# Expert rows in units of 128, two experts split ahead, narrow blocks interleaved, O's low half ahead of the maxima

## Chip, cores and metric

The kernel runs on one core of one Trainium2 chip. The metric is the device time of one execution in microseconds. The engines are PE (matmul; PEld its weight loads), DVE, ACT, POOL and SP; each works through its own queue in order, and semaphores join them. DMAs are issued from the queues of SP, ACT and POOL.

## What is computed

For x of 4 batches x 1024 tokens x 256, the reference adds to x an attention output times a gate that a mixture of experts makes. Both start from the same normalized input.

```python
x = L0_attn_x
xn = _layernorm(x)
s = attention(xn)              # 8 heads of 128, one shared K and V, causal, position added to q and k
logits = xn @ router_w + router_b          # 8 experts, the two largest are kept
gating = softmax(kept logits)
h = relu(einsum('td,edh->eth', xn, w1) + b1)      # H = 1024
y = einsum('eth,ehd->etd', h, w2) + b2
g = silu(einsum('etd,te->td', y, gating))
return x + s * g
```

Only the two chosen experts of a token count, so the kernel gathers rows by expert: 4096 tokens x 2 = 8192 rows.

## The kernel before

Every float32 operand of a large product is split in two float16 halves, high and low (PASSES: high x high, high x low, low x high), so each product of 128 x 128 weights is three matmuls.

`prologue` (lines 300 to 750) loads x in pairs of tiles (p = 0 to 15, two tiles of 128 tokens each). Per pair, DVE normalizes, ACT makes the high half, POOL (even p) or DVE (odd p, BY_DVE) the low half, PE turns both and makes the router's logits, and ACT or DVE (six p, OUT_DVE) copies the turned tile out of PSUM. In the second half of this loop ACT and POOL also scale and split the weights of expert 0 (`weights`, 8 pieces of 128 x 512). Then comes the routing, all on DVE and PE in one chain: `choose` twice (the two largest logits), `counts` on PE (33 matmuls that leave in psR for each token the number of rows of each expert ahead of it, and the totals), `blocks` (blocks of each expert and where they start), `ranks` and `slots` (a row number for each token and choice), `one_hots` with `place` on PE (the inverse: which token stands in each row), `owners` (blk_e, the expert of each block), and who, the list of tokens by row. A block has BLK = 256 rows of one expert, and 39 blocks (NBLK) are enough for any counts. POOL then gathers 128 rows at a time (`gather`, an indirect DMA), SP turns the first four (`straight`) and stores the others (`keep`) in a table in memory, from where ACT later loads them turned (`load`). A part ends when all engines have passed its end, POOL's drain (a wait for its own work) among them.

`experts` (lines 756 to 912) takes the blocks in order. For block n and each of 8 groups g of 128 hidden units, PE runs `up(n, g)` and `down(n - 1, g)`, six matmuls each, ACT adds the bias and makes relu, DVE splits the result, and DVE and ACT bring out the rows of block n - 2. The weights of the block's expert are addressed through a register that is loaded from blk_e, and PE waits for w_done (8 pieces for each expert) at a block's start. POOL alternates one gather and the split of one piece (`split`: scale, high, low); SP alternates `keep` and `stage` (the piece's load). AHEAD = 8 gathers lie in the prologue.

`attention` (lines 915 to 1424) has 32 heads of five steps k. In each step PE makes the scores of a group of query tiles and, from the previous head, one of four `values` (the product with V, in two PSUM banks by turns), and sometimes a projection (a job) or an output tile. DVE does reciprocals(k-1), maxima(k), the low half of a job, `o_low` (the low half of a values result, which frees its bank), and `low(k-2)` of the probabilities. ACT does a job's high half, exponentials, and `o_high`, the high half of a values result, ahead of `o_low`.

## Time and profile before

| | us |
|---|---|
| median of 3 runs | 1158.84 (1158.31 to 1159.88) |
| profiled execution | 1160.2 |
| its span | 1158.4 |
| PE busy in it | 1041.3 (90%) |
| DVE busy | 889.6 (77%) |
| ACT busy | 553.7 (48%) |
| POOL busy | 521.3 (45%) |

The busy shares are means over three parts with different limits, so they are read by stretch. All readings are from one execution; the difference between its time and its span, 1.8 us, lies around the program. A time of the trace counts from the span's start. The form "[0.61 <-DVE b_outs L1276]" behind a row is the idle time of its engine just before it, and what ended it.

### The profile page before, as it was taken

Reading aid. Unit: us, or ns where it says so; the run is one execution under the profiler, and the core shown is the slowest. Engines: PE = TensorE matmul, PEld = TensorE weight load, DVE = VectorE, ACT = ScalarE, POOL = GpSimd, SP = SyncE. Lnnn points to the kernel's source line nnn. Section 1 sums busy time; section 2 is a strip of 40 time slices with the busy share of each in tenths; the row PEclk is TensorE's granted clock in tenths of the full one; section 3 lists DMA queues with packets and bytes.
Section 4 is the critical chain, followed back from the end, with each engine's and each line's share of the span. In section 5 each row is a group of like instructions: output and inputs, shape, how many; then the busy total and the mean of one; then the engine's idle time right before and its main releaser. Section 6 shows DMA issues by size and latency. Waiting matters only on the chain.

```text
span 1158.4 us, 28653 instructions
## 1 busy us (share of the span) xinstructions
PE 1041.3 (90%) x10419; PEld 839.2 (72%) x10419; DVE 889.6 (77%) x1570; ACT 553.7 (48%) x1251; POOL 521.3 (45%) x546
## 2 busy tenths in 40 slices
PE   2554999999999999998888989999999999999997
PEld 1443888888888888875666667767777677767776
DVE  7772676777666644448989999998989898999981
ACT  3701233323333333326666766665656665756640
POOL 1506999999986500002333334332434333434441
PEclk9966999999999999999999999999999999999999
DMA  7336578766666732226998999988899879999994
GB/s 267 115 140 169 160 178 177 180 170 174 178 177 152 142 66 56 47 74 93 165 150 143 147 159 169 164 146 150 143 179 174 147 141 152 150 166 158 156 172 107
DMA packets 412137, 172.41 MB, mean 149 GB/s; under 512 B 352730, under 2 KB 402212, under 8 KB 411364
## 3 DMA queue, kind: packets, MB, share of 16 engines
q1 hardware_dynamic: 350064, 127.97, 56.5%
q10 hardware_dynamic: 55124, 23.99, 9.2%
q0 software_dynamic: 6816, 18.62, 8.5%
q8 instruction: 90, 1.47, 0.6%
q14 instruction: 43, 0.35, 0.1%
HBM read 52.29 MB, written 32.51 MB: 73 GB/s over the span
## 4 chain that ended last, share of the span: by engine, by line
DVE 27%; PE 21%; ACT 2%; DMA 2%; issue 2%; SPq 0%; ACTq 0%; DVEq 0%
DVE b_nmax L1229 9%; DVE b_ph L1268 8%; PE b_psO L1052 7%; PE b_psS L1033 5%; PE b_psJ L1066 5%; DVE b_outs L1276 3%; DVE b_psJ L1238 2%; DMA b_pT<-b_ph 2%; DVE b_Q L1252 2%; PE b_psS L1077 2%; PE b_psS L990 2%; ACT b_ph L1164 1%; DVE b_f L1282 1%; ACT b_pr L1132 1%; PE b_psJ L990 1%
## 5 line engine op out<-in xcount | busy, mean ns | idle before, releaser
L1357 POOL TENSOR_SCALAR b_ph<-b_pr,b_rrec 128x896 f16<-128x896 f32 (+4 forms) x160 | 136.3, 859 | 469.4 <-DVE b_rrec L1258 446.0
L861 ACT ACTIVATE h<-psU,bias 128x256 f32<-128x256 f32 x312 | 129.1, 471 | 317.6 <-PE psU L809 193.7
L809 PE MATMUL psU<-bxT,w_p 128*128 128x256 f16 x1872 | 255.7, 274 | 17.8 <-issue 17.8
L1132 ACT ACTIVATE b_pr<-b_psS,b_nmax 128x1024 f32<-128x1024 f32 (+7 forms) x256 | 187.0, 735 | 142.6 <-DVE b_nmax L1229 139.2
L822 PE MATMUL psY<-w_p,hp 128*128 x1872 | 254.1, 273 | 0.0
L1052 PE MATMUL b_psO<-b_pT,b_vp 128*128 128x128 f16 x3456 | 216.1, 220 | 37.0 <-DVE b_outs L1276 26.4
L1052 PEld LDWEIGHTS b_psO<-b_pT,b_vp 128*128 128x128 f16 x3456 | 198.3, 98 | 52.5 <-DVE b_outs L1276 37.8
L879 DVE CAST hp<-h 128x512 f16<-128x512 f32 x156 | 98.0, 628 | 158.0 <-ACT h L861 147.7
L1033 PE MATMUL b_psS<-b_kp,b_Q 128*128 128x512 f16 (+3 forms) x1152 | 218.7, 326 | 0.1
L809 PEld LDWEIGHTS psU<-bxT,w_p 128*128 x1872 | 183.9, 98 | 40.2 <-issue 18.3
L1268 DVE SCALAR_TENSOR_TENSOR b_ph<-b_pr,b_rrec,b_ph 128x1024 f16<-128x1024 f32 (+7 forms) x256 | 208.0, 843 | 0.0
L1229 DVE TENSOR_REDUCE b_nmax<-b_psS 128x1 f32<-128x1024 f32 (+7 forms) x256 | 182.1, 742 | 25.3 <-PE b_psS L1036 25.3
L822 PEld LDWEIGHTS psY<-w_p,hp 128*128 128x128 f16 x1872 | 183.2, 98 | 21.2
L1033 PEld LDWEIGHTS b_psS<-b_kp,b_Q 128*128 128x128 f16 x1152 | 103.1, 98 | 77.8 <-issue 1.0
L881 DVE TENSOR_TENSOR hp<-h,hp 128x512 f16<-128x512 f32 x156 | 140.2, 899 | 5.4
L153 POOL DMA_INDIRECT rowx<-xn_split,who x78 | 86.6, 1111 | 56.7 <-DVE who L697 30.5
...
L1164 ACT ACTIVATE b_ph<-b_pr,b_rrec 128x1024 f16<-128x1024 f32 (+2 forms) x96 | 78.7, 853 | 2.0 <-DVE b_rrec L1258 2.0
L225 POOL TENSOR_TENSOR w_p<-wstage,w_p 128x512 f16<-128x512 f32 x56 | 74.4, 1329 | 4.8
L1154 ACT ACTIVATE b_Q<-b_psJ,bias 128x512 f16<-128x512 f32 x59 | 40.5, 687 | 63.2 <-DVE b_psJ L1238 62.4
L1276 DVE SCALAR_TENSOR_TENSOR b_outs<-b_psO,bias,b_outs 128x256 f16<-128x256 f32 x128 | 60.5, 473 | 12.6 <-ACT b_outs L1141 12.5
L1141 ACT ACTIVATE b_outs<-b_psO,bias 128x256 f16<-128x256 f32 x128 | 60.3, 471 | 19.7 <-PE b_psO L1052 19.6
(169 smaller groups left out, 1032.7 us busy)
## 6 DMA issues: line engine op xcount, KB each, us to landing
...
b_pT<-b_ph SPq DMA_TRANSPOSE x256
...
```

Source lines behind the costliest of these rows:

```text
L809: mm = eng.matmul(psU[w % U][:, g % 2, :].rearrange("p (t r) -> p t r", t=2), weight(n, a * W1 + c * H + g * P, P), bxT[n % 3][:, :, 2 * b ...
L822: mm = eng.matmul(psY[n % 2][:, t, :], hp[n % 2][:, a, g, t * P:(t + 1) * P], weight(n, 2 * W1 + (2 * g + b) * D, D), start=(g == 0 and k ...
L861: a = eng.activation(h32[w % 4][:, g, :], psU[w % U][:, g, :], ACT.Relu, bias=bias[:, ds(e * HT + 2 * q + g, 1)], scale=1.0 / WS)
L879: eng.tensor_copy(hp[n % 2][:, 0, sl, :], h32[w % 4][:, :, :]).then_inc(hh_, 1)
L881: eng.tensor_tensor(hp[n % 2][:, 1, sl, :], h32[w % 4][:, :, :], hp[n % 2][:, 0, sl, :], ALU.subtract).then_inc(hl_, 1)
L1033: mm = eng.matmul(dst, Q[n % 3][:, a, u * P:(u + 1) * P], kb[:, c, lo:lo + w], start=(kk == 0), stop=(kk == 2 and not last))
L1052: mm = eng.matmul(psO[w % 2][:, (u % 2) * P:(u % 2 + 1) * P], vb[:, a, j, :], pT[u][:, c * (u + 1) + j, :], start=(j == 0 and kk == 0), st ...
L1132: a = eng.activation(pr[k % 3][:, o:o + w], psS[BUF[i]][:, :, :].rearrange("p a n -> p (a n)")[:, o:o + w], ACT.Exp, bias=nmax[:, at:at + ...
L1229: a = eng.tensor_reduce(nmax[:, at:at + 1], psS[BUF[i]][:, :, :].rearrange("p a n -> p (a n)")[:, o:o + w], AX.X, ALU.max, negate=True)
L1268: a = eng.scalar_tensor_tensor(ph[k % 4][:, 2 * o + w:2 * o + 2 * w], pr[k % 3][:, o:o + w], rrec[:, at:at + 1], ph[k % 4][:, 2 * o:2 * o ...
L1276: eng.scalar_tensor_tensor(o[:, 1], psO[(4 * n + s) % 2][:, 0:2 * P], bias[:, B_V:B_V + 1], o[:, 0], ALU.add, ALU.subtract).then_inc(al_, 1)
L1357: a = eng.tensor_scalar(ph[k % 4][:, 2 * o:2 * o + w], pr[k % 3][:, o:o + w], rrec[:, at:at + 1], 1.0, ALU.mult, ALU.mult)
```

## The change

- Rows come in units of 128. An expert's rows are cut in pairs of units (blocks of 256), and a rest of 1 to 128 rows is one single unit. All pairs come first in expert order (TWIN = 31 slots), then all singles. There are 71 units and NBLK = 40 blocks, 31 of 256 rows and 9 of 128. `blocks`, `ranks` and `owners` do the arithmetic for this. Where there are more than 31 pairs, the rest are two single units each.
- `counts`: two matmuls give the totals by tile, DVE copies them, and three matmuls with a table (tri16) give the same numbers as the 33.
- Low halves of x are all DVE's, and ACT copies all turned tiles but two. The weights of experts 0 and 1 are split in the prologue and just behind it: ACT makes the high halves behind the loop, DVE the low halves (`first_low`), eight behind who and eight at the start of `experts`. POOL's splits begin with expert 2 (FIRST = 16).
- `slots` handles both choices at once, and the eight one-hots follow in a row; `gates` goes ahead of `blocks`.
- Four gathers and two turned loads stay in the prologue; the others open the expert part. The load of block 2 follows block 0's relu.
- `narrow(n, g)`: in narrow blocks two up matmuls (128 columns) alternate with one down matmul of the block before. The expert registers of these are loaded ahead, two in a block.
- In `attention`, `o_low` stands ahead of `maxima`.

```diff
-    NBLK = 2 * N // BLK + E - 1
-    UNITS = NBLK * BLK // P
-    C_TH, C_BL = C_E + E, C_E + E + MOST
-    C_LN, C_TK = C_BL + UNITS, C_BL + UNITS + P
-    CW = C_TK + NT
+    TWIN = N // P - 1
+    UNITS = 2 * N // P + E - 1
+    NBLK = UNITS - TWIN
...
+    def units_of(n):
+
+        return (2 * n, 2 * n + 1) if n < TWIN else (n + TWIN,)
+
+    def loaded(n):
+
+        return sum(16 * len(units_of(k)) for k in range(2, n + 1) if k % 3 == n % 3)
...
+    def first_low(eng, q):
+
+        hi, lo, _ = halves(q)
+        eng.wait_ge(wh0_, q + 1)
+        eng.scalar_tensor_tensor(lo, raw_of(q), WS, hi, ALU.mult, ALU.subtract).then_inc(wd_, 1)
...
-    BY_DVE = tuple(p for p in range(TWOS) if p % 2)
-    OUT_DVE = tuple(p for p in range(TWOS) if p % 8 in (1, 4, 6))
+    OUT_DVE = (TWOS - 3, TWOS - 1)
...
-                eng.matmul(psR[:, 0:NT * E], up16[:, :], M16[:, :], start=True, stop=False)
-                eng.matmul(psR[:, NT * E:], one16[:, :], M16[:, 0:E], start=False, stop=False)
-                for m in range(NT):
-                    to = NT + (m > 0)
-                    mm = eng.matmul(psR[:, (m + 1) * E:to * E].rearrange("p (n e) -> p n e", e=E), one16[:, :],
-                                    M16[:, m * E:(m + 1) * E].unsqueeze(1).to_broadcast([P, to - m - 1, E]),
-                                    start=False, stop=(m == NT - 1))
-                mm.then_inc(s_cnt, 1)
+                for h in range(PARTS):
+                    mm = eng.matmul(psJ[:, h * P:(h + 1) * P], M16[:, h * P:(h + 1) * P], one16[:, :], start=True, stop=True)
+                mm.then_inc(s_tot, 1)
+                eng.wait_ge(s_tab, 4)
+                eng.wait_ge(s_t16, 1)
+                for h in range(PARTS):
+                    eng.matmul(psR, tot16[:, h * P:(h + 1) * P], tri16[:, h, :], start=(h == 0), stop=False)
+                eng.matmul(psR[:, 0:NT * E], up16[:, :], M16[:, :], start=False, stop=True).then_inc(s_cnt, 1)
...
-                hi, _, rows = halves(q)
-                full = w_raw[:, q, :]
-                if rows:
-                    full = full.rearrange("p (g d) -> p g d", d=rows)
-                eng.activation(hi, full, ACT.Copy, scale=WS).then_inc(s_wh, 1)
-                eng.activation(full, full, ACT.Copy, scale=WS).then_inc(s_ws, 1)
-
-            eng.dma_start(c_sb[:, :], cst).then_inc(s_c, 16)
+                eng.activation(halves(q)[0], v["raw_of"](q), ACT.Copy, scale=WS).then_inc(wh0_, 1)
...
-                    if p >= 8:
-                        weights(p - 8)
...
+            for q in range(PIECES):
+                weights(q)
             eng.wait_ge(s_diff, 1)
             eng.activation(ex[:, 0, :], ex[:, 2, :], ACT.Exp).then_inc(s_e, 1)
+            for q in range(PIECES, 2 * PIECES):
+                weights(q)
             eng.dma_start(pe_sb[:, :], pe).then_inc(s_pe, 16)
...
-                if p - 1 in BY_DVE:
+                if 0 <= p - 1 < TWOS:
...
+                for j in range(2):
+                    link(eng.tensor_tensor(cm[:, j], c_sb[:, C_TH + j * MOST:C_TH + (j + 1) * MOST].unsqueeze(1).to_broadcast([P, E, MOST]),
+                                           cnt.unsqueeze(2).to_broadcast([P, E, MOST]), ALU.is_lt))
+                link(eng.tensor_reduce(nbl[:, :, :], cm, AX.X, ALU.add))
+                link(eng.tensor_tensor(nbl[:, 0, :], nbl[:, 0, :], nbl[:, 1, :], ALU.subtract))
...
+                step(eng.scalar_tensor_tensor(slot[:, :, :], row(se[0][:, 1, :]), float(BLK), rank, ALU.mult, ALU.add))
+                link(eng.tensor_tensor(cand[:, :, :], rank, row(lim[:, :]), ALU.is_ge))
+                link(eng.tensor_tensor(cand[:, :, :], cand[:, :, :], row(move[:, :]), ALU.mult))
+                link(eng.scalar_tensor_tensor(slot[:, :, :], cand[:, :, :], float(P), slot[:, :, :], ALU.mult, ALU.add))
...
+            eng.wait_ge(s_tot, 1)
+            eng.tensor_copy(tot16[:, :], psJ[:, 0:PARTS * P]).then_inc(s_t16, 1)
+            gates()
             blocks()
             ranks()
-            slots(0)
-            eng.wait_ge(s_tab, 3)
-            for s in range(CHUNKS // 2):
-                one_hots(s)
-            slots(1)
-            for s in range(CHUNKS // 2, CHUNKS):
+            slots()
+            eng.wait_ge(s_tab, 4)
+            for s in range(CHUNKS):
                 one_hots(s)
             owners()
-            gates()
             eng.wait_ge(s_sp, 1)
             eng.tensor_scalar(who[:, :], psJ[:, 0:UNITS], float(T * 2), None, ALU.add).then_inc(v["who_"], 1)
+            for q in range(PIECES):
+                v["first_low"](eng, q)
...
-            for n in range(v["AHEAD"]):
+            for n in range(4):
...
+            for n in range(2):
                 v["straight"](eng, n)
-            for n in range(4, v["AHEAD"]):
-                v["keep"](eng, n)
...
+            for n in range(2, 4):
+                v["straight"](eng, n)
+            for n in range(4, AHEAD):
+                v["keep"](eng, n)
             eng.dma_start(b2b[:, :], b2.rearrange("e d -> (e d)").partition_broadcast(P)).then_inc(b_l, 16)
-            p = PIECES + 2
-            for n in range(AHEAD, UNITS):
+            for n in range(AHEAD, AHEAD + 4):
+                v["keep"](eng, n)
+            p = FIRST + 2
+            for n in range(AHEAD + 4, UNITS):
...
+            def narrow(n, g):
+
+                w = PAIR * n + g // 2
+                if g % 2 == 0:
+                    eng.wait_ge(rl_, w - U + 1)
+                    eng.wait_ge(hl_, w - PAIR + 1)
+                for k in range(3 * DC):
+                    a, b = PASSES[k // DC]
+                    c = k % DC
+                    mm = eng.matmul(psU[w % U][:, g % 2, 0:P], weight(n, a * W1 + c * H + g * P, P), bxT[n % 3][:, 0, 2 * b + c, :],
+                                    start=(k == 0), stop=(k == 3 * DC - 1))
+                    if k == 3 * DC - 1 and g % 2:
+                        mm.then_inc(up_, 1)
+                    if k % 2:
+                        a, b = PASSES[k // 2]
+                        mm = eng.matmul(psY[(n - 1) % 2][:, 0, :], hp[(n - 1) % 2][:, a, g, 0:P],
+                                        weight(n - 1, 2 * W1 + (2 * g + b) * D, D),
+                                        start=(g == 0 and k == 1), stop=(g == HT - 1 and k == 3 * DC - 1))
+                if g == HT - 1:
...
+                    if TWIN < n < NBLK:
+                        narrow(n, g)
+                    elif n < NBLK:
                         up(n, g)
-                    if n:
+                    if n and n <= TWIN:
                         down(n - 1, g)
-                    if g == PAIR and n + 1 < NBLK:
-                        es.append(expert(eng, n + 1))
+                    elif n == NBLK and g % 2:
+                        down(n - 1, g // 2)
+                    known = min(NBLK, n + 2 + max(0, n + 11 - TWIN))
+                    if g in (2, PAIR) and len(es) < known - (g == 2):
+                        es.append(expert(eng, len(es)))
...
+                if n == 0:
+                    v["load"](eng, 2)
...
+            for q in range(PIECES, FIRST):
+                v["first_low"](eng, q)
...
-            p = PIECES
-            for n in range(AHEAD, UNITS):
+            for n in range(4, AHEAD + 4):
                 v["gather"](eng, n)
-                if p == 2 * PIECES:
-                    eng.wait_ge(v["xk_"], 48)
+            p = FIRST
+            eng.wait_ge(wd_, FIRST)
+            eng.wait_ge(v["xk_"], 48)
+            for n in range(AHEAD + 4, UNITS):
+                v["gather"](eng, n)
...
+                if k <= LAST and (k - 1) // 5 >= 1 and (k - 1) % 5:
+                    o_low((k - 1) // 5 - 1, (k - 1) % 5 - 1)
                 if k < LAST:
                     maxima(k)
                 if k - 1 in jobs.at:
                     job_low(jobs.at[k - 1])
-                if k <= LAST and (k - 1) // 5 >= 1 and (k - 1) % 5:
-                    o_low((k - 1) // 5 - 1, (k - 1) % 5 - 1)
...
```

PE's queue in the expert part, before, a piece within a block (psU is the up product, psY the down product; ISA is a register operation for the weights' address):

```order
L809 ISA
L809 MATMUL psU<-bxT_66,w_p 128x256 x3
L809 ISA
L809 MATMUL psU<-bxT_66,w_p 128x256
L809 ISA
L809 MATMUL psU<-bxT_66,w_p 128x256
L822 ISA
L822 MATMUL psY<-w_p,hp_1104 128x256
L822 ISA
L822 MATMUL psY<-w_p,hp_1104 128x256 x2
L822 ISA
L822 MATMUL psY<-w_p,hp_1104 128x256
```

After, in a narrow block:

```order
L886 ISA
L886 MATMUL psU<-bxT_67,w_p 128x128
L886 ISA
L886 MATMUL psU<-bxT_67,w_p 128x128
L892 ISA
L892 MATMUL psY<-w_p,hp_1078 128x256
L886 MATMUL psU<-bxT_67,w_p 128x128 x2
L892 ISA
L892 MATMUL psY<-w_p,hp_1078 128x256
L886 ISA
L886 MATMUL psU<-bxT_67,w_p 128x128
L886 ISA
```

The down matmul of the block before now stands behind every second up matmul, and the up matmuls have half the columns.

POOL's queue around the end of the prologue, before (rowx are the gathered rows, wstage and w_p the piece of weights before and behind the split; the two branches are the end of one part and the start of the next):

```order
L153 DMA rowx_64<-xn_split,who 128x512
L153 DMA rowx_61<-xn_split,who 128x512
L153 DMA rowx_62<-xn_split,who 128x512
L153 DMA rowx_63<-xn_split,who 128x512
L153 DMA rowx_64<-xn_split,who 128x512
L303 UNCONDITIONAL_BRANCH
L902 UNCONDITIONAL_BRANCH
L153 DMA rowx_61<-xn_split,who 128x512
L221 ISA
L221 TENSOR_SCALAR wstage_59<-wstage_59 128x512
L223 CAST w_p<-wstage_59 128x512
L225 TENSOR_TENSOR w_p<-wstage_59,w_p 128x512
```

After:

```order
L171 DMA rowx_62<-xn_split,who 128x512
L171 DMA rowx_63<-xn_split,who 128x512
L171 DMA rowx_64<-xn_split,who 128x512
L339 UNCONDITIONAL_BRANCH
L985 UNCONDITIONAL_BRANCH
L171 DMA rowx_61<-xn_split,who 128x512
L171 DMA rowx_62<-xn_split,who 128x512
L171 DMA rowx_63<-xn_split,who 128x512
L171 DMA rowx_64<-xn_split,who 128x512
L171 DMA rowx_61<-xn_split,who 128x512
L171 DMA rowx_62<-xn_split,who 128x512
L171 DMA rowx_63<-xn_split,who 128x512
```

Four gathers moved behind the end, and eight gathers stand ahead of the first split.

DVE's queue in a head of the attention part, before, the third and fourth of its five steps (b_nmax are the maxima, b_outs the low half of O, b_ph the low half of the probabilities, b_Q that of a projection):

```order
L1258 RECIPROCAL b_rrec<-b_rsum 128x2
L1229 TENSOR_REDUCE b_nmax<-b_psS 128x1 x2
L1252 SCALAR_TENSOR_TENSOR b_Q_22317<-b_psJ,bias,b_Q_22317 128x512
L1276 SCALAR_TENSOR_TENSOR b_outs_22333<-b_psO,bias,b_outs_22333 128x256
L1268 SCALAR_TENSOR_TENSOR b_ph_22319<-b_pr_22344,b_rrec,b_ph_22319 128x896
L1268 SCALAR_TENSOR_TENSOR b_ph_22319<-b_pr_22344,b_rrec,b_ph_22319 128x128
L1258 RECIPROCAL b_rrec<-b_rsum 128x2
L1229 TENSOR_REDUCE b_nmax<-b_psS 128x1
L1276 SCALAR_TENSOR_TENSOR b_outs_22333<-b_psO,bias,b_outs_22333 128x256
L1268 SCALAR_TENSOR_TENSOR b_ph_22320<-b_pr_22342,b_rrec,b_ph_22320 128x768
```

After:

```order
L1343 RECIPROCAL b_rrec<-b_rsum 128x2
L1361 SCALAR_TENSOR_TENSOR b_outs_22547<-b_psO,bias,b_outs_22547 128x256
L1314 TENSOR_REDUCE b_nmax<-b_psS 128x1 x2
L1337 SCALAR_TENSOR_TENSOR b_Q_22531<-b_psJ,bias,b_Q_22531 128x512
L1353 SCALAR_TENSOR_TENSOR b_ph_22533<-b_pr_22558,b_rrec,b_ph_22533 128x896
L1353 SCALAR_TENSOR_TENSOR b_ph_22533<-b_pr_22558,b_rrec,b_ph_22533 128x128
L1343 RECIPROCAL b_rrec<-b_rsum 128x2
L1361 SCALAR_TENSOR_TENSOR b_outs_22547<-b_psO,bias,b_outs_22547 128x256
L1314 TENSOR_REDUCE b_nmax<-b_psS 128x1
L1353 SCALAR_TENSOR_TENSOR b_ph_22534<-b_pr_22556,b_rrec,b_ph_22534 128x768
```

The low half of O moved from behind the maxima and the projection to the place behind the reciprocals.

## Rows read from the trace of the kernel before

**Rows 1.** Busy time by stretch, three parts: us, PE, PEld, DVE, ACT, POOL, clock, DMA.

```profile
0.00:103.27 103.27, 36.33 (x420) 31.54 (x420) 65.45 (x174) 33.59 (x59) 27.70 (x31) 0.83 0.51 169
...
103.27:513.90 410.63, 410.55 (x3744) 367.02 (x3744) 257.16 (x350) 129.11 (x312) 255.69 (x265) 1.00 0.57 139
...
513.90:1158.40 644.50, 594.44 (x6256) 440.68 (x6256) 566.97 (x1046) 390.97 (x880) 237.94 (x251) 0.99 0.90 152
```

**Rows 2.** PE in time (start, us, engine, line): matmuls by width, register operations.

```profile
54.03 0.83 PE L412 MATMUL a_psX<-a_rw_p,a_xT 128*128 128x8 f16 x24
...
737.93 1.35 PE L1052 MATMUL b_psO<-b_pT,b_vp 128*128 128x128 f16 x21 [0.61 <-DVE b_outs L1276]
...
739.11 2.78 PE L1066 MATMUL b_psJ<-b_wo,b_outs 128*128 128x256 f16 x24
...
741.73 1.46 PE L1033 MATMUL b_psS<-b_kp,b_Q 128*128 128x512 f16 x6
...
L809 PEldq FUSED_REGOPS  x1248: 46/46/51, 103.2 to 505.8; - x179
```

**Rows 3.** POOL, the line that ends the split of one piece of weights.

```profile
L225 POOL TENSOR_TENSOR w_p<-wstage,w_p x56: 1152/1394/1482, 105.1 to 339.9; 128x512 f16<-128x512 f32 x56
```

**Rows 4.** Timeline of DVE and ACT, second half of the normalization loop.

```profile
38.59 0.68 DVE L566 TENSOR_TENSOR a_xp<-a_x_all,a_xp 128x512 f16<-128x512 f32 x1
...
39.19 1.37 DVE L560 TENSOR_SCALAR a_x_all<-a_x_all,a_mv,a_rs 128x256 f32<-128x256 f32 x4
...
45.09 3.52 DVE L560 TENSOR_SCALAR a_x_all<-a_x_all,a_mv,a_rs 128x256 f32<-128x256 f32 x4
...
47.16 0.63 ACT L460 ACTIVATE a_xp<-a_x_all 128x512 f16<-128x512 f32 x1 [0.63 <-DVE a_x_all L560]
...
48.59 0.62 ACT L472 ACTIVATE w_p<-a_w_raw 128x512 f16<-128x512 f32 x1
...
55.87 0.42 DVE L590 SCALAR_TENSOR_TENSOR a_L<-a_psX,a_rbb 128x256 f32<-128x256 f32 x1 [2.12 <-PE a_psX L412]
```

**Rows 5.** Timeline of the routing, from the counts to who.

```profile
62.16 3.65 PE L426 MATMUL a_psX<-a_M,a_one 128*128 128x248 f16 x32
...
65.85 0.17 DVE L615 COPY a_nbl<-a_psX 128x8 f32<-128x8 f32 x1 [3.97 <-PE a_psX L426]
...
68.26 0.42 DVE L632 TENSOR_TENSOR a_cand<-a_oh,a_slot 128x256 f32<-128x256 f32 x1
...
85.77 0.23 DVE L697 TENSOR_SCALAR who<-a_psJ 128x78 uint32<-128x78 f32 x1
```

**Rows 6.** Timeline from the gathers to the first expert matmul; POOL's drain.

```profile
90.82 0.94 POOL L153 DMA_INDIRECT rowx<-xn_split,who  x1 [0.30 <-issue]
...
95.08 0.94 POOL L153 DMA_INDIRECT rowx<-xn_split,who  x1 [0.78 <-DMA bxT<-rowx]
...
97.58 0.95 POOL L153 DMA_INDIRECT rowx<-xn_split,who  x1 [0.30 <-issue]
...
103.27 7.63 PE L809 MATMUL psU<-bxT,w_p 128*128 128x256 f16 x54 [17.82 <-issue]
...
L303 POOLq DRAIN  x1: 4706/4706/4706, 96.9 to 96.9; - x1
```

**Rows 7.** Three heads by stretch; two rows of one head; DVE's waits from 600 to 1100.

```profile
559.93:577.09 17.16, 15.41 (x165) 10.87 (x164) 16.60 (x32) 11.88 (x27) 7.24 (x7) 1.00 1.00 159
...
724.97:743.28 18.31, 17.70 (x189) 13.22 (x188) 17.11 (x32) 11.89 (x27) 7.47 (x9) 1.00 1.05 158
...
743.28:763.49 20.21, 19.01 (x195) 13.83 (x194) 18.50 (x35) 12.46 (x28) 7.37 (x9) 1.00 0.86 150
...
731.49 0.47 ACT L1141 ACTIVATE b_outs<-b_psO,bias 128x256 f16<-128x256 f32 x1
...
731.64 0.17 DVE L1258 RECIPROCAL b_rrec<-b_rsum 128x2 f32<-128x2 f32 x1 [0.56 <-ACT b_pr L1132]
...
DVE b_nmax L1229 <- PE b_psS L1036: 23.0, 36, 1.1
```

214 lines of the change are left out of this document (122 added, 92 removed).

## The prediction

> **What bounds the kernel now.** I read the stretches first [rows 1]. The program has three parts in a row: a prologue of 103.3 us, an expert part of 410.6 us, an attention part of 644.5 us. In the expert part PE is busy 410.55 of 410.63 us: it is bound by PE alone, and every column of matmul taken out there is time taken out, until another engine comes late. In the prologue no engine is full (DVE 65 of 103 us), so its length is a chain of waits. In the attention part PE (92%) and DVE (88%) share the bound, and the waits between them count. The profiled execution took 1160.2 us with a span of 1158.4; the median of the runs is 1158.84. I take the differences from the trace and subtract them from the median.
>
> **Expert part.** Before, the 8192 (token, expert) pairs lie in 39 blocks of 256 rows. Each costs 48 up and 48 down matmuls of 256 columns. The spacing of such matmuls is (741.73 - 739.11)/24 = 0.1092 us [rows 2], so a block is 96 x 0.1092 = 10.48 us, and 39 are 408.8 us; the 1.8 us left of 410.6 is the slow clock of the first block. After, there are 31 blocks of 256 and 9 of 128 rows. A narrow block has 48 up matmuls of 128 columns and 24 down matmuls of 256 (128 rows instead of 256). For 128 columns with new weights each time the trace has 21 matmuls in 739.11 - 737.93 = 1.18 us, or 0.0562 us each [rows 2]. Narrow block: 48 x 0.0562 + 24 x 0.1092 = 5.32 us. Sum after: 31 x 10.48 + 9 x 5.32 = 372.8, plus 1.8: 374.6. **Gain 36.0 us**; I take 35, for seams.
>
> Can PE's queue feed narrow matmuls? Their addresses depend on the expert's number, and between them stand register operations of 46 ns [rows 2], four for six up matmuls, two more for three down ones: 6 x 0.046 = 0.28 us for each of the eight groups of a narrow block. The nine matmuls with their weight loads take the queue at most 9 x 0.035 us (24 pairs of 8 columns in 0.83 us [rows 2]) = 0.31. Together 0.59, against 0.66 us of streaming: just hidden, and the change alternates two narrow and one wide matmul, so that the load is even. The trace shows no such mix at 128 columns. Its bounds: all of the 0.28 us hidden, 5.3 us a block; none of it hidden, 5.32 + 8 x 0.28 = 7.6 us, or 20 us more for nine blocks. I take the first, since in blocks of 256 columns eight operations a group leave the spacing at 0.109.
> The Trainium skill, page "TensorE: Matmul & The Clock Gate", section "Back-to-back issue gap", speaks against this: it gives about 81 ns for each matmul of 128 columns in a stream of weight load and matmul, and 56 ns only for one alone. This trace's stream [rows 2] runs at 56 ns with a load for each matmul, so for the stream without register operations the measurement decides. By the page's figure the 432 narrow up matmuls would cost 432 x 0.025 = 10.7 us more and the gain be 25 us, an estimate from that page.
>
> Other engines in a narrow block: half of the elements for ACT and DVE, one transpose to issue instead of two; they had slack at 10.5 us and keep it at 5.3. The weights are what could come late. POOL splits one piece per 4.27 us (56 pieces, 105.1 to 339.9 [rows 3]); an expert has 8. Counting the reference's two largest logits gives 949, 679, 619, 1082, 885, 639, 2114, 1225 rows, so 31 pairs of units: 4, 3, 2, 4, 3, 2, 8, 5. Expert 6 now begins in block 18 and not in 22, at about 2 + 18 x 10.48 = 190.6 us after PE's start. POOL has 5 experts (2 to 6) to split by then, since two come split: 40 x 4.27 = 170.8 us, begun after the gathers and the wait for w_done, about 12 us after PE's start: ready at 183. **No stall, 8 us in hand**; the other experts have 16 us or more. PE's wait for w_done, if late, would hold all of up and down behind it.
>
> **Prologue up to the row numbers (who).** (a) All low halves move from POOL and DVE to DVE (8 more x 0.68 us), four of six copies out of PSUM from DVE to ACT, and ACT's weight work out of the loop. Before, the second half of the loop runs at ACT's step: high half and copy 48.59 - 47.16 = 1.43 us, and two weight operations behind them [rows 4]; and DVE is held when POOL reads (four normalizations 3.52 us beside POOL, 1.37 alone [rows 4]). After, a step is ACT's 1.43, and DVE's 0.69 + 0.60 (two normalizations, one low half) fits under it. The loop's half starts near 35 (as before, perhaps 0.5 later by the extra lows) and takes 8 x 1.43 plus 3 us to drain: logits at 50 and not at 55.87 [rows 4]. Gain 6 (bounds 3 and 7).
> (b) The 33 counting matmuls (PE 62.16, next DVE 65.85 [rows 5]) take 4.0 us from the mask to the counts; after, two matmuls, a copy of 256 columns (0.42) and three matmuls, about 1.7. Gain 2.3. (c) More arithmetic: in blocks() one compare, a 256-wide reduction and four small ones, +1.0; in ranks() three 256-wide ones, 3 x 0.45 = +1.3; in owners() +0.9; gates() moves beside the counts, -0.7; slots() once 2.35 instead of twice 1.79, -1.2; eight one-hots over 568 instead of 624 columns, -0.6. These are worked out from 0.42 us for an operation of 256 columns and 0.17 for a small one [rows 5], with 0.03 between them. Net +0.7. (a) to (c): **who 7.6 us earlier**, at 78 and not 86.
>
> **From who to the first expert matmul**, 17.3 us before (86.0 to 103.27 [rows 5, 6]). Eight gathers go ahead of the part's end; the last is 97.58 to 98.53, POOL's drain lasts to 101.6 [rows 6], then 1.7 us to the matmul. So 4.74 us lie behind the last gather. After, four gathers: the fourth ended at 91.76, 5.8 us after who. PE starts 5.8 + 4.74 = 10.5 us after who. **Gain 6.8.** DVE's eight low halves of expert 0 come behind who: 8 x 0.61 = 4.9, under the gathers. The two transposes that block 0 needs landed by 95.1, 9.1 after who, under the drain. If that drain is no fixed cost, the transposes bound it and the gain is 8.1; if moved work holds, 4. Moved behind the start, in their queues' order: on SP two transposes and four keeps; on POOL gathers 4 to 11 ahead of all splits; on ACT the load of block 2, behind block 0 (issued 8.5 us after PE's start, landed by 14, needed at 17); on DVE eight low halves of expert 1, 5 us, ahead of the first split (needed 7 us after the start; ready at 5.5). All hidden, the last two by 2 to 3 us. Prologue in all: 7.6 + 6.8 = **14.4 us** (bounds 9 and 18).
>
> **Attention.** o_low moves ahead of maxima. In a usual head (18.31 us, PE 17.70 busy [rows 7]) DVE waits twice: about 0.60 for the scores ahead of the widest maxima (23.0 us in 36 such waits), 0.56 for ACT's exponentials [rows 7]. PE waits 0.61 for o_low ahead of the 21 matmuls [rows 2], which is why the scores are late. Following one head in the new order: at the widest maxima o_low (0.39) runs inside the 0.60 wait, and that wait itself shrinks, since PE waits no more; this saves 0.60 of idle time. New waits: behind the 0.56 wait, reciprocals end at 731.71, but ACT's high half of O ends at 731.96 [rows 7]: o_low starts 0.29 later, and everything after it too; at the fourth group the same costs 0.07. So 0.60 becomes about 0.2 net: a head takes 17.9, still over PE's 17.7. In the eight heads of 20.2 us DVE waits for scores a second time [rows 7], and o_low fits in that too: -0.7 each. In four early heads of 17.16 us [rows 7] with no wait for scores the order only costs, +0.36 each. Sum: 13 x -0.38, 8 x -0.7, 4 x +0.36 = **-9 us**. Bounds: -14 (all 36 waits filled by 0.39), and +3 for the case that the wait for ACT's high half of O comes in most steps.
>
> **Sum:** 1158.8 - 35 - 14.4 - 9 = **1100.4**; I say 1101.
>
> **Rivals.** (1) Narrow matmuls bound by PE's queue: half of the register time shows, 72 groups x 0.14 = 10 us, 1111; all of it, 1121. For it: ten to fifteen instructions in 0.66 us, a density that no row shows; against: the count above. (By the page's 81 ns the time would be 1112.) (2) The new order in attention gains nothing, because each o_low waits for ACT: 1110 to 1113. For it: the 0.25 us seen above; against: the waits for scores in 21 heads. (3) Weights late: POOL's step of 4.27 us has to pass (190.6 - 12)/40 = 4.47 before expert 6 is late; each 0.1 us more costs 4 us. 4.6 gives 1106. POOL's steps lie between 3.8 and 4.7 now. (4) **Slower than before** by the same mechanism: needs a step of 4.47 + 58/40 = 5.9 us, 1160 or more. DVE's casts hold POOL's work, and the part's blocks are not shorter in the wide stretch, so nothing raises the step by 38%; but gathers, keeps and loads of weights go through the same queues. (5) The change doesn't do what it says: fewer blocks of 256, but PE waits for rows between narrow blocks (transposes and gathers at 5.3 us a block): if each took 10.5, the gain of the expert part would vanish and 1136 remain. Units are gathered one per 4.27 us from early on, some 40 us ahead at block 31.
>
> **How the numbers follow.** Forecast 0.60, (1) 0.15, (2) 0.13, (3) 0.06, (4) 0.03, (5) 0.03. The range takes in (1) and (2) alone, and on the other side the prologue's 18 with attention's 14: 1101 - 4 - 5 - 1 = 1091, with a margin 1089; upward (1) at 1111 with most of (2), 1119. About 0.2% (2.3 us) is what a measurement tells from no change; nothing but (4) comes near it. Faster 0.96, same 0.01, slower 0.03.
>
> **What would show it.** In the profile after: the first expert matmul at 88 to 90; PE full from there for 375 us; a narrow block's spacing of 5.3 (or 6.5) us; no PE wait at block 18; last expert matmul near 464; heads of 17.9 and 19.5 us and no PE wait for b_outs. I am wrong if PE's stretch shows idle time, if the drain of POOL grows, or if heads stay at 18.3.

## The result, and the profile after the change

| | before | after |
|---|---|---|
| median of the runs, us | 1159.36 (1158.31 to 1162.2) | 1115.96 (1113.58 to 1122.9) |
| ratio | | 0.9632 (95% 0.9582 to 0.9681) |
| profiled execution, span, us | 1158.4 | 1121.1 |
| to the first expert matmul | 103.27 | 90.18 |
| expert part, to the end of its last matmul | 410.6 | 391.6 |
| from there to the end | 644.5 | 639.3 |

Forecast were 1101 us, range 1089 to 1119. Run again beside other kernels the same program took 1113.53 us (0.9586 of before, 0.9574 to 0.9598). Its profile had a span of 1114.1 with the same three stretches at 88.5, 390.7 and 634.9. The first profile lies 7 us above that, 4.4 of them in the attention part. I read mechanisms from both, and sizes from the repeated runs where they exist.

After, busy time by stretch (us, then PE, PEld, DVE, ACT, POOL, clock, share of the DMA engines, GB/s), as [rows 1]:

```profile
0.00:90.18 90.18, 32.82 (x391) 27.98 (x391) 69.54 (x197) 37.42 (x64) 5.63 (x11) 1.00 0.61 203
90.18:481.80 391.62, 387.12 (x3624) 339.22 (x3624) 242.76 (x366) 125.13 (x320) 233.61 (x238) 1.00 0.54 135
...
483.26:1121.10 637.84, 596.91 (x6256) 444.70 (x6256) 570.77 (x1045) 391.94 (x880) 203.51 (x251) 0.98 0.88 153
```

Before, PE had 0.1 us of idle time in the expert part; now it has 4.5, and that is only a part of what is missing. The rest hides in a PE that counts as busy. Three windows of 3 us in the narrow blocks, which begin at 425.11:

```profile
425.00:428.00 3.00, 3.00 (x43) 2.84 (x41) 0.72 (x2) 0.84 (x4) 0.00 (x0) 1.00 0.42 112
428.00:431.00 3.00, 2.87 (x36) 2.39 (x33) 2.24 (x6) 1.50 (x6) 0.00 (x0) 1.00 0.08 25
...
434.00:437.00 3.00, 3.00 (x34) 2.34 (x33) 1.84 (x6) 1.74 (x6) 0.00 (x0) 1.00 0.22 73
```

PE is "busy" in all of them, but 43 matmuls start in the first and 34 in the third. A matmul's record is longer than its place in the stream (0.22 to 0.27 us for a spacing of 0.056 to 0.109), so gaps of 0.1 to 0.2 us don't show as idle time. Only the count, or the spacing of starts, shows them. The eight narrow blocks from 425.11 to 478.98 take 53.9 us, 6.74 each, where 5.32 was forecast.

The start of the expert part, PE's queue in time (6 matmuls of 256 columns take 0.66 us at full clock), and its clock there:

```profile
107.09 0.82 PE L871 MATMUL psY<-w_p,hp 128*128 x6
111.53 1.46 PE L858 MATMUL psU<-bxT,w_p 128*128 128x256 f16 x6 [3.62 <-DMA bxT<-expert_rows]
112.78 1.49 PE L871 MATMUL psY<-w_p,hp 128*128 x6
114.06 1.02 PE L858 MATMUL psU<-bxT,w_p 128*128 128x256 f16 x6
...
110.00:114.00 4.00, 2.47 (x12) 1.83 (x13) 3.90 (x6) 0.90 (x3) 2.73 (x4) 0.63 1.18 199
```

PE waits 3.6 us for the rows of block 2, and from 110 to 114 us, around the end of that wait, the granted clock is 0.63 on average, a mix of its two levels of 1.2 and 2.4 GHz: the first twelve matmuls behind the wait take twice their time, and with the next six that is some 1.4 us more.

The attention part: one early, one usual and one long head, as [rows 7]; then what waits there. The maxima of DVE (L1314) wait 8.6 us for scores where it was 25, and PE's waits for b_outs are gone.

```profile
528.18:545.76 17.58, 15.64 (x170) 11.15 (x168) 16.82 (x33) 11.90 (x27) 5.37 (x8) 1.00 1.02 164
676.13:694.17 18.04, 17.70 (x190) 13.23 (x189) 17.24 (x34) 11.90 (x27) 6.07 (x9) 1.00 0.98 165
752.57:772.09 19.52, 19.04 (x214) 14.58 (x213) 17.94 (x35) 12.39 (x28) 6.09 (x9) 1.00 0.85 149
...
PE b_psO L1137 <- DMA b_pT<-b_ph: 20.4, 17, 2.8
...
DVE b_nmax L1314 <- PE b_psS L1121: 8.6, 13, 1.8
```

### The profile page after: what moved, and what is told of

Read it like the earlier page. It is cut to its first block, busy times and chain, and to the rows that moved or that the text cites. A ratio compares the mean times of both kernels' runs of the same rounds, so it can differ in the third digit from the quotient of the medians.

```text
span 1121.1 us, 28441 instructions
## 1 busy us (share of the span) xinstructions
PE 1016.8 (91%) x10270; PEld 811.9 (72%) x10270; DVE 883.5 (79%) x1607; ACT 554.5 (49%) x1264; POOL 442.7 (39%) x499
## 4 chain that ended last, share of the span: by engine, by line
DVE 27%; PE 20%; ACT 4%; issue 3%; DMA 2%; SPq 1%; ACTq 0%; DVEq 0%
DVE b_ph L1353 10%; DVE b_nmax L1314 8%; PE b_psO L1137 7%; PE b_psS L1118 5%; DVE b_outs L1361 2%; PE b_psJ L1075 2%; PE b_psJ L1151 2%; DVE b_psJ L1323 2%; ACT b_pr L1217 2%; PE b_psS L1162 2%; DMA b_pT<-b_ph 2%; ACT b_ph L1249 1%; PE b_psS L1075 1%; DVE b_Q L1337 1%; DVE b_f L1367 1%
## 5 line engine op out<-in xcount | busy, mean ns | idle before, releaser
L1442 POOL TENSOR_SCALAR b_ph<-b_pr,b_rrec 128x896 f16<-128x896 f32 (+4 forms) x160 | 109.3, 691 | 502.3 <-DVE b_rrec L1343 460.6
L938 ACT ACTIVATE h<-psU,bias 128x256 f32<-128x256 f32 (+1 forms) x320 | 125.1, 448 | 294.5 <-PE psU L858 170.4
L1137 PE MATMUL b_psO<-b_pT,b_vp 128*128 128x128 f16 x3456 | 219.1, 221 | 20.5 <-DMA b_pT<-b_ph 20.4
L858 PE MATMUL psU<-bxT,w_p 128*128 128x256 f16 (+1 forms) x1536 | 208.3, 273 | 16.5 <-DVE w_p L261 12.8
L871 PE MATMUL psY<-w_p,hp 128*128 x1512 | 206.4, 273 | 0.0
L959 DVE CAST hp<-h 128x512 f16<-128x512 f32 (+1 forms) x160 | 85.9, 537 | 137.1 <-ACT h L938 135.0
L1314 DVE TENSOR_REDUCE b_nmax<-b_psS 128x1 f32<-128x1024 f32 (+7 forms) x256 | 183.3, 748 | 8.6 <-PE b_psS L1121 8.6
L858 PEld LDWEIGHTS psU<-bxT,w_p 128*128 x1536 | 150.1, 99 | 35.6 <-issue 17.4
L871 PEld LDWEIGHTS psY<-w_p,hp 128*128 128x128 f16 x1512 | 147.8, 98 | 17.4
L961 DVE TENSOR_TENSOR hp<-h,hp 128x512 f16<-128x512 f32 (+1 forms) x160 | 134.8, 843 | 5.5
L171 POOL DMA_INDIRECT rowx<-xn_split,who x71 | 80.4, 1132 | 106.7 <-DVE who L755 78.3
L1151 PE MATMUL b_psJ<-b_wo,b_outs 128*128 128x256 f16 x576 | 66.8, 273 | 2.1 <-DVE b_G L1382 2.1
L250 POOL TENSOR_TENSOR w_p<-wstage,w_p 128x512 f16<-128x512 f32 x48 | 63.0, 1313 | 4.1
```

The costliest lines, as they stand in the source:

```text
L858: mm = eng.matmul(psU[w % U][:, g % 2, 0:tiles * P].rearrange("p (t r) -> p t r", t=tiles), weight(n, a * W1 + c * H + g * P, P), bxT[n % ...
L871: mm = eng.matmul(psY[n % 2][:, t, :], hp[n % 2][:, a, g, t * P:(t + 1) * P], weight(n, 2 * W1 + (2 * g + b) * D, D), start=(g == 0 and k ...
L938: a = eng.activation(h32[w % 4][:, g, 0:rows], psU[w % U][:, g, 0:rows], ACT.Relu, bias=bias[:, ds(e * HT + 2 * q + g, 1)], scale=1.0 / WS)
L961: eng.tensor_tensor(lo, full, hi, ALU.subtract).then_inc(hl_, 1)
L1137: mm = eng.matmul(psO[w % 2][:, (u % 2) * P:(u % 2 + 1) * P], vb[:, a, j, :], pT[u][:, c * (u + 1) + j, :], start=(j == 0 and kk == 0), st ...
L1151: mm = eng.matmul(psJ[:, 0:D], outs[b % many][:, a, h, t * P:(t + 1) * P], wo_p[:, e, h, :], start=(h == 0 and kk == 0), stop=(h == HEADS ...
```

## The experiments

Ratios are to the kernel before, run on the same chip in the same rounds.

| run | median us | ratio (95%) |
|---|---|---|
| after_again | 1113.53 | 0.9586 (0.9574 to 0.9598) |
| static_narrow | 1103.8 | 0.9502 (0.9489 to 0.9515) |
| static_downs | 1103.54 | 0.951 (0.9485 to 0.9536) |
| order_back | 1125.27 | 0.9694 (0.9661 to 0.9728) |
| before_order | 1149.64 | 0.9894 (0.9878 to 0.991) |
| gathers_8 | 1121.5 | 0.9659 (0.9633 to 0.9685) |
| b2_late | 1117.62 | 0.9615 (0.9593 to 0.9637) |
| early_splits | 1114.23 | 0.9596 (0.9576 to 0.9617) |
| mixed | 1110.14 | 0.9558 (0.9544 to 0.9572) |
| mixed_early | 1110.47 | 0.9564 (0.9541 to 0.9587) |
| mixed_early_g2 | 1115.48 | 0.9596 (0.9546 to 0.9647) |
| mixed_load3 | 1106.87 | 0.9543 (0.9526 to 0.956) |

**The changed kernel again.** 

> The changed kernel once more, so that the next three have it beside them on one chip. 1113 to 1118 us expected. In the profile of its first run a narrow block (128 rows) took 6.74 us where 5.32 was forecast, PE waited 3.6 us for the rows of block 2, and PE waited 20.4 us (17 waits) for transposed probabilities in the attention part. If these waits for the transposes are a matter of the single execution, this profile shows another number of them (before had 10.4 us in 12); if they belong to the new order of the attention part, it shows 20 us again.

Measured: PE's wait for transposed probabilities is 20.0 us in 14 waits, so it belongs to the new order. The other profiles bear it out: all twelve with the new order have 18.9 to 22.5 us of it, the two with the old one 10.4 and 15.6. The wait for block 2's rows is 2.5 us, and a new one of 0.5 us for weights stands at block 18.

### What bounds the narrow blocks

**Constants in place of the lookup.**

```diff
             def weight(n, off, width):
+                if n >= TWIN:
+                    at = min(n - TWIN + 2, E - 1) * WE + off
+                    return w_p[:, at:at + width]
                 return w_p[:, ds(es[n] * WE + off, width)]
```

> The changed kernel, with the expert of the nine narrow blocks written into PE's program as a constant (2, 3, 4, 5, 6 and four times 7) and not looked up: PE's six register operations per group are gone there, ACT's and DVE's stay. This leaves out PE's part of the routing for those blocks, so the program holds for these inputs alone. Theory A (PE's queue bounds the narrow blocks: their matmuls run at 0.22 us per three until the queue's lead is used up, then at 0.84 us a group): the group falls to 0.66 us, a narrow block from 6.74 to 5.3, the stretch of eight shrinks by 11 us, 1103 to 1106 us. Rival B (something in the data path, such as PSUM or reads of rows beside ACT and DVE, holds the alternation of narrow and wide matmuls): the group stays at 0.84 us and the time at 1113 to 1118. Half (5 us) would say that both take part.

Measured: -9.7 us against the changed kernel, the 0.9502 clear of its interval. The eight narrow blocks, from the first row of their up matmuls:

```profile
L889 PE MATMUL psU<-bxT,w_p x384: 216/219/219, 426.7 to 470.6; 128*128 128x128 f16 x192
```

Start to start this is 43.9 us instead of 53.7, with 1.3 us of waits in it: 5.3 us a block. Theory A holds and B falls.

**Constants for the down matmuls only**, two of six register operations a group. 

> The changed kernel with constants in place of the looked-up expert for the down matmuls of the narrow groups alone: four register operations a group are left of six. This leaves out that part of the routing, so it holds for these inputs alone. It measures what one register operation costs PE's queue. With six the group takes 0.84 us, with none it streams in 0.66. If one costs the 46 ns that its record shows, the group takes 0.84 - 0.09 = 0.75 us and the stretch of eight narrow blocks 48 us; if one costs twice that, about 0.09 us, the group is back at 0.66 and the stretch at 42.5 us. If the queue is bound by something else than these operations (and the first run with constants had its gain by chance of the places), it stays near 54 us.

Measured: 1103.54 us (two runs), the whole gain with four operations left. The records of the register operations on PE's queue and of the matmuls that they serve, first of the changed kernel, then of this run (both: count, ns, first and last start):

```profile
L886 PE MATMUL psU<-bxT,w_p x384: 219/219/228, 425.1 to 478.8; 128*128 128x128 f16 x192
L886 PEldq FUSED_REGOPS  x256: 46/46/46, 423.9 to 478.6; - x128
```

```profile
L889 PE MATMUL psU<-bxT,w_p x384: 218/220/228, 422.1 to 465.5; 128*128 128x128 f16 x192
L889 PEldq FUSED_REGOPS  x256: 46/46/46, 420.8 to 464.3; - x128
```

This is the mechanism in two lines. At the first narrow block the queue is 1.2 us ahead of PE in both. In the changed kernel the lead is gone by the end (0.2 us), so PE has nothing left to work from but what the queue hands out at that moment. With two operations fewer the queue keeps its 1.2 us. A full group takes 53.9/64 = 0.84 us on average (the first ones still live on the lead) and one with four operations at most 0.66, so one costs at least (0.84 - 0.66)/2 = 0.09 us, twice its record of 46 ns. Taking the prediction's 0.31 us (its upper bound) for the nine matmuls, (0.84 - 0.31)/6 = 0.088 says the same. This is the price that leaves with an operation; whether a part of it lies in the instruction that takes its address from the operation, no run separates. The Trainium skill, page "Perfetto Trace Analysis", section "Sequencer-only Instruction (DRAIN, etc)", says that the profiler shows only the execution of such an instruction and not its decode or the hand-over to the next. The trace agrees: 46 ns are recorded and at least 90 are paid.

**Narrow among wide blocks.** The lookup stays; the order of the blocks changes from the 25th on.

```diff
+    ORDER = list(range(TWIN - 7)) + [b for j in range(7) for b in (TWIN - 7 + j, TWIN + j)] + [TWIN + 7, TWIN + 8]
...
-        return (2 * n, 2 * n + 1) if n < TWIN else (n + TWIN,)
+        b = ORDER[n]
+        return (2 * b, 2 * b + 1) if b < TWIN else (b + TWIN,)
```

(`narrow` is used where two narrow ones meet, else `up` and `down`; the number of the expert is read from blk_e at b.)

> The changed kernel with the narrow blocks not all at the end: from the 25th block on wide and narrow ones alternate (seven of each), then the last two narrow ones. No work is left out, the routing is looked up as before. Theory A from the runs so far (constants in place of the lookup gave -9.7 us): PE's queue needs 0.84 us for a narrow group that streams in 0.66, and about 1.1 us for a wide one that streams in 1.31, so beside a wide block a narrow one hides its register operations: of the 11 us some 8 come back, 1105 to 1108, with seven of the nine narrow blocks at their streaming time. Rival: the queue can't run ahead by enough (its lead was 1.2 us at block 31, a narrow block falls 1.4 us behind): a third comes back, 1110 to 1112. Rival: the rows of the narrow blocks are gathered last (unit 62 at about 325 us, its load is asked for at 326) and come late for an order in which they stand earlier: 1114 or more, with waits for rows.

Measured: 1110.14 us, an interval below the changed kernel's. The expert part of the profile is 383.1 us against 390.7, so up to 7.6 of the 11 us come back, near the 8 of theory A. (The unchanged expert part took 388.1 in order_back's profile, so the gain may be as small as 5.) A narrow block after a wide one, each row six up matmuls of it, with six wide down matmuls between:

```profile
352.65 0.50 PE L863 MATMUL psU<-bxT,w_p 128*128 128x128 f16 x6
...
353.64 0.50 PE L863 MATMUL psU<-bxT,w_p 128*128 128x128 f16 x6
...
354.63 0.50 PE L863 MATMUL psU<-bxT,w_p 128*128 128x128 f16 x6
```

The spacing of 0.99 us is 6 x 0.0562 + 6 x 0.1092: full streaming. The whole time gained only 3.4 us, which is in the range of the first rival (a third comes back) and not of theory A. In the profiles the attention part took 2.3 us longer (637.2 against 634.9) and the prologue 0.9. The spacing shows the mechanism of theory A; why the whole time gained less stays open.

### The order in the attention part

**Undone in the changed kernel.** 

> The changed kernel with the low half of O put back behind the maxima on DVE in the attention part; all else as changed. If the new order gains what the prediction took (9 us), this is 9 us slower than the changed kernel: 1123 to 1126, and PE waits for b_outs come back (26 us in 35 waits), a usual head 18.3 us. If it gains about 5, the difference of the two attention parts in the first pair of profiles, 1119 to 1121. If the 5 us come from elsewhere (the start of the part), 1114 to 1116.

**Done alone in the kernel before.**

```diff
+                if k <= LAST and (k - 1) // 5 >= 1 and (k - 1) % 5:
+                    o_low((k - 1) // 5 - 1, (k - 1) % 5 - 1)
                 if k < LAST:
                     maxima(k)
                 if k - 1 in jobs.at:
                     job_low(jobs.at[k - 1])
-                if k <= LAST and (k - 1) // 5 >= 1 and (k - 1) % 5:
-                    o_low((k - 1) // 5 - 1, (k - 1) % 5 - 1)
```

> The kernel before with one thing changed: the low half of O ahead of the maxima on DVE. The prediction's term of the sum by itself: -9 us, 1150 (0.992). Rival: the gain is about 5 us, 1154 (0.996), since the four early heads lose 0.4 each and transposes of the probabilities come late more often. If nothing, 1159.

Measured: +11.7 us when undone and -11.4 us when done alone: the same from both sides, and more than the 9 forecast. The waits in the kernel before:

```profile
PE b_psO L1052 <- DVE b_outs L1276: 26.4, 35, 1.2
DVE b_nmax L1229 <- PE b_psS L1036: 25.3, 38, 1.5
...
PE b_psO L1052 <- DMA b_pT<-b_ph: 10.4, 12, 2.3
```

Those in the changed kernel with the order undone (order_back), and in the kernel before with the new order alone (before_order):

```profile
PE b_psO L1137 <- DVE b_outs L1361: 25.2, 32, 1.2
...
PE b_psO L1137 <- DMA b_pT<-b_ph: 15.6, 12, 2.7
```

```profile
PE b_psO L1052 <- DMA b_pT<-b_ph: 21.0, 18, 2.5
...
DVE b_nmax L1229 <- PE b_psS L1036: 5.0, 10, 0.8
```

In both pairs 25 us of PE's waits for DVE vanish, and 4 us (15.6 against after_again's 20.0) to 11 us (10.4 against 21.0) of new ones for transposes appear.

### The first 20 us of the expert part

**Eight gathers ahead of the boundary.** 

> The changed kernel with eight gathers (and two more transposes and four keeps) ahead of the part's boundary instead of four, as the kernel before has it. The prediction's step: POOL's drain is a fixed cost behind the last gather, so the first expert matmul comes 4 x 1.25 us plus what the gathers wait for a free buffer later: 95 to 97 instead of 88.5 to 90.2. Then PE waits for no rows of block 2, and POOL's first split starts no later than now. Time by the step: +6 to 7 at the start, -2 to -3 at block 2, so 1117 to 1119. Rival: the length from who to the first matmul is set by something else (DVE's eight low halves of weights, the transposes): less than 3 us later, 1113 to 1115.

Measured: the first matmul at 97.09, 8.6 us later than in after_again at the same who (78.3), and 1121.5 us. The step stands. From the end of the last gather to the first matmul it took 4.5 us here, 5.5 and 3.7 in the two profiles of the changed kernel, around the 4.74 forecast. PE waited for no rows.

**b2 fetched later.** 

> The changed kernel with one DMA on SP's queue moved: the biases b2 (1 MB written, 10.6 us in the profile) are fetched behind the keeps of units 8 to 11 and not ahead of them. Theory C: the wait of PE for the rows of block 2 (3.6 and 2.5 us in two profiles, none or 0.6 in two others) comes from that transfer, which shares the DMA engines with the transposes of block 2: the wait falls to 0.5 or less, POOL's waits for the keeps (12 and 9 us) shrink by half, its first split starts by 105 and not 108 to 112, and the time is 1111 to 1113. Rival: the rows are late because their gathers start only behind the part's boundary: the wait stays at 2 to 4 us and the time at 1113 to 1116.

Measured: this profile has no wait for rows and POOL's first split begins at 100.95, but that doesn't show theory C. The profile of order_back, with the expert part as changed and b2 fetched early, has no wait for rows either and its first split at 104.90. The time is 1117.62, not better. PE has 3.4 us of other waits at 97 to 105 instead, 1.8 of them for DVE's halves of h:

```profile
104.25 0.84 PE L871 MATMUL psY<-w_p,hp 128*128 x6 [1.80 <-DVE hp L961]
```

**Splits earlier.**

```diff
-            for n in range(4, AHEAD + 4):
+            for n in range(4, AHEAD):
                 v["gather"](eng, n)
```

> The changed kernel with POOL's first split of weights behind gather 8 and not behind gather 11: gathers 8 to 11 and their keeps alternate with splits, as all later ones do. The prediction had the splits begin 12 us after PE's start and expert 6 ready 8 us ahead of need; the profiles show 18 to 22 us (gathers 8 to 11 wait for buffers that the keeps free) and, in two of four, PE waiting for that expert's weights (0.5 and 2.9 us, block 18). If that is the cause, the first split starts by 102, no profile shows the wait at block 18, and the time is 1 to 2 us less, 1111 to 1113. Rival: the wait comes from POOL's step (4.1 to 4.7 us, held by the DMA of weights), not from its start: the wait stays and so does the time, 1113 to 1115.

Measured: first split at 94.57, no wait for weights or rows, expert part 387.5 us (order_back's, without this edit, 388.1); and 0.9596 can't be told from 0.9586. Theory and rival stay undecided.

**Both edits.** 

> Both helpful edits together: narrow and wide blocks alternate from the 25th on, and POOL's splits begin behind gather 8. mixed alone gave 0.9558 of before (expert part 383.1 us in its profile, with 1.9 us of waits of PE at 97 to 101 us), the early splits alone an expert part of 387.5 us against 390.7 to 391.6. Expected: an expert part of 380 to 382 us, no PE wait for weights or rows, 0.952 to 0.955 of before, about 1107 us. Rival: the early waits only change their place (rows, weights or PE's own instructions, all in the first 20 us, when the DMA engines are full), and the time is mixed's, 1110.

Measured: 1110.47, mixed's time. The waits did change their place, but not within the first 20 us as the rival had it. ACT, its queue, and PE at 341 us:

```profile
335.04 1.27 ACTq L203 DMA_TRANSPOSE bxT<-expert_rows  x1
...
338.65 1.57 ACT L942 ACTIVATE h<-psU,bias 128x256 f32<-128x256 f32 x4 [9.27 <-issue]
...
341.76 0.85 PE L861 MATMUL psU<-bxT,w_p 128*128 128x256 f16 x6 [2.22 <-issue]
```

ACT stands 9.3 us behind the load of the first narrow block. Its unit, number 62, is gathered at 329.20 here and at 318.23 in mixed: with four splits moved ahead of it, POOL now comes to the splits of wo, which wait for buffers, before it gathers that unit. This is the rival named for mixed.

**Two gathers ahead of the boundary.** 

> As mixed_early, with two gathers ahead of the part's boundary instead of four (block 0 needs only units 0 and 1). Eight instead of four made the start 6 to 8 us later. If the boundary follows the last gather, the first expert matmul comes 2.5 us earlier, at 85 to 86.5; the rows of blocks 1 and 2 come as before in absolute time, so PE waits for them up to 2.5 us: between -2.5 and 0 against mixed_early. Rival: with two gathers the bound is DVE's eight low halves of expert 0 (they end 5.1 us after the row numbers) or the transposes of block 0 (9 us after them): the first matmul stays at 88 to 89.

Measured: the first matmul came at 86.47, 2.4 us earlier than in mixed_early (88.90), but PE then waited 4.2 us at 341, for the same load of unit 62, and 1.5 us at 116. Four runs spread from 1105.8 to 1120.7: inconclusive as a time.

**The load of block 3.** What all these profiles share is a gap on ACT. In the first profile after, its last relu of block 0 and its first of block 1, and what stands between them on its queue:

```profile
97.76 1.38 ACTq L199 DMA_TRANSPOSE bxT<-expert_rows  x1
97.94 0.47 ACT L938 ACTIVATE h<-psU,bias 128x256 f32<-128x256 f32 x1
99.24 7.87 ACTq L199 DMA_TRANSPOSE bxT<-expert_rows  x3
107.86 2.67 ACT L938 ACTIVATE h<-psU,bias 128x256 f32<-128x256 f32 x7 [9.46 <-PE psU L858]
```

The loads wait for the keeps of units 4 to 7, whose gathers now come behind the boundary, and every relu of block 1 stands behind them.

```diff
                     a.then_inc(rl_, 1)
+                    if n == 1 and q == 2:
+                        v["load"](eng, 3)
                 if n == 0:
                     v["load"](eng, 2)
-                if n + 3 < NBLK:
+                if 0 < n < NBLK - 3:
                     v["load"](eng, n + 3)
```

> mixed, with the load of block 3's rows (two transposes on ACT's queue, each behind a wait for the keep of its unit) asked for in the middle of block 1 and not at the end of block 0. In all profiles after the change ACT stands still for 4.3 to 9.5 us between its last relu of block 0 and its first of block 1, at 97 to 108 us, with the loads of blocks 2 and 3 ahead of that relu on its queue; DVE and then PE wait behind it (PE 1.9 us in mixed, 3.6 in the first profile after). Theory D: the load of block 3 holds the relus of block 1: the gap shrinks to 1 to 4 us (the load of block 2 is still ahead of it), PE's idle time before 125 us falls under 1 us, and the time is mixed's less 1 to 2 us, 0.954 to 0.955 of before. Rival: the gap is the load of block 2 (its keeps come late because their gathers start behind the part's boundary): gap and time stay, 0.956.

Measured: 1106.87 us, the fastest full program of this study, 52.8 us under the kernel before. The gap on ACT is 2.81 us; it was 5.29 in mixed and 5.7 to 9.5 in the others. PE shows no idle time from its start to 125. In mixed its idle time was 1.9 us at 98 to 101, ahead of ACT's gap and not behind it, and from 102 to 125 it counted as busy for 23.00 us there too, with 200 matmuls at a granted clock of 0.94 against the 213 below. Weights are late at block 18:

```profile
102.00:125.00 23.00, 23.00 (x213) 20.62 (x212) 12.54 (x18) 8.00 (x20) 17.49 (x20) 1.00 0.91 172
...
279.27 1.20 PE L863 MATMUL psU<-bxT,w_p 128*128 128x256 f16 x6 [3.18 <-POOL w_p L254]
```

It is expert 6, whose weights POOL has split by then and no sooner. The interval (0.9526 to 0.956) overlaps mixed's, so that this edit gains time is not shown. That the load of block 3 made a part of ACT's gap is shown by the shorter gap; that the gap cost PE time in mixed is not. With the earlier splits it wasn't run.

## Why the prediction was right or wrong

**The sum.** Forecast 1100.4, measured 1113.5 to 1116. The three terms, in the profile of after_again: prologue -14.8 (forecast -14.4), experts -19.9 (forecast -36.0, -35 taken), attention -9.6 (forecast -9; by the paired runs -11.5). One term was wrong, by 15 us: the main forecast of 1101 failed, and the range held the time because it took in rival (1). In part that was luck. The wait for block 2's rows with the slow clock behind it, 5 us in the first profile, was in no rival; it fell in the room that the range had for rival (2), which didn't come.

**Prologue, right step by step.** ACT's step of the loop is 1.42 us (forecast 1.43) and DVE fits under it; the logits are there at 49.35 (forecast 50); who at 78.12 (forecast 78):

```profile
43.23 1.05 ACT L506 ACTIVATE a_xT<-a_turn 128x1024 f16<-128x1024 f16 x1
44.13 0.67 ACT L502 ACTIVATE a_xp<-a_x_all 128x512 f16<-128x512 f32 x1
44.65 1.06 ACT L506 ACTIVATE a_xT<-a_turn 128x1024 f16<-128x1024 f16 x1
...
49.35 0.42 DVE L631 SCALAR_TENSOR_TENSOR a_L<-a_psX,a_rbb 128x256 f32<-128x256 f32 x1 [0.58 <-PE a_psX L454]
...
78.12 0.23 DVE L755 TENSOR_SCALAR who<-a_psJ 128x71 uint32<-128x71 f32 x1
```

From there to the first matmul it was 12.05 us in the first profile and 10.2 in the second; forecast 10.5. The drain behind the last gather is the bound, as gathers_8 shows.

**Experts: the step "just hidden" failed.** I counted 6 x 0.046 + 9 x 0.035 = 0.59 us of queue against 0.66 of streaming. The 0.046 was the length of a record, not what the operation costs its queue; it costs 0.09, the queue needs 0.84, and narrow blocks take 6.74 us. That is 8 x 1.42 = 11.3 us. Rival (1) had the mechanism and the size ("half of the register time shows", 10 us), with a chance of 0.15 that was too low. My argument against it, that eight operations a group leave the spacing at 0.109 in wide blocks, was no evidence: by the cost found here that queue needs 12 x 0.035 + 8 x 0.09 = 1.14 us, under 1.31. It fits either price. In static_narrow 48 matmuls of 128 columns and 24 of 256 take 5.3 us, so a narrow one takes 56 ns, as the trace of the kernel before said. The Trainium skill, page "TensorE: Matmul & The Clock Gate", section "Back-to-back issue gap", gives 81 ns, which would have forecast nearly the time that was measured, but for a reason that this run excludes.

**Experts: "all hidden, the last two by 2 to 3 us" failed too.** Block 2's rows were forecast for 14 us behind PE's start and needed at 17; PE waited for them until 21. The wait cost 3.6 us and the slow clock behind it some 1.4. With 374.6 + 11.3 + 3.6 + 1.4 = 390.9 the measured 391.6 is accounted for. The step that failed is the time from issue to landing: the two transposes were issued 7.6 and 9.1 us after PE's start (forecast 8.5), but the rows had landed only 21.3 us after it, not 14. Why they took so long is open, and they don't always: of the twelve profiles from the change on three have this wait, 3.6, 2.5 and 0.6 us. I had also not looked at who stands behind a waiting load on ACT's queue, the relus of block 1; but the wait of 3.6 us ended with the rows' landing, by the trace, and not with a relu.

**Weights: right outcome, wrong margin.** I gave expert 6 "8 us in hand", with POOL's splits beginning 12 us after PE's start. They began 22 us after it (112.21), since gathers 8 to 11 waited 11.9 us for buffers that the keeps had to free. POOL's steps of about 4.1 us made up for part. There was no wait in the first profile, but 0.5, 2.9 and 3.2 us in three others: the margin is nil.

**Attention: right mechanism, a little small.** Usual heads 18.04 (forecast 17.9), long ones 19.52 (19.5), early ones 17.58 (17.52). The waits for scores fell from [rows 7]'s 23.0 us in 36 (600 to 1100) to 6.8 in 10 (600 to 1060). By the shared runs the order is worth 11.4 to 11.7 us. By class, 13 usual, 8 long and 4 early heads give -7.4. The rest may lie in two heads that I had left out of the classes, 21.6 and 19.2 us before and 18.2 and 18.0 in before_order. The first of them, in the kernel before and in before_order:

```profile
594.25:615.84 21.59, 18.17 (x171) 13.11 (x170) 18.31 (x35) 12.68 (x28) 6.88 (x7) 0.92 0.67 133
```

```profile
598.47:616.71 18.24, 16.37 (x170) 11.52 (x170) 18.04 (x34) 12.47 (x28) 6.04 (x8) 1.00 0.87 146
```

In the old order PE waits there 2.2 us for a transpose and 1.2 for b_outs, and the 45 matmuls behind the first wait take 4.30 us; in the new order it waits 1.6 us for a transpose, and they take 2.67. So 1.6 of the 3.4 us are a slow clock, and that this belongs to the order isn't shown. The same explains most of the first profile's -5.2 in place of -9.6. Three of its heads have slow matmuls behind a wait for a transpose:

```profile
564.51 4.30 PE L1137 MATMUL b_psO<-b_pT,b_vp 128*128 128x128 f16 x45 [1.99 <-DMA b_pT<-b_ph]
...
603.05 4.05 PE L1137 MATMUL b_psO<-b_pT,b_vp 128*128 128x128 f16 x45 [2.75 <-DMA b_pT<-b_ph]
...
659.36 3.86 PE L1137 MATMUL b_psO<-b_pT,b_vp 128*128 128x128 f16 x45 [2.38 <-DMA b_pT<-b_ph]
```

That is 4.2 us over 3 x 2.67. In after_again one head has it, 1.2 us, though PE's waits for transposes are as long in total (20.0 us against 20.4). There, matmuls behind a wait of 2.69 us ran at full clock:

```profile
655.61 2.67 PE L1137 MATMUL b_psO<-b_pT,b_vp 128*128 128x128 f16 x45 [2.69 <-DMA b_pT<-b_ph]
```
